# Fused expert product and quantized product: the stores of the results move from SyncE's queue to one of GpSimd's

## What is computed

```
cond = einsum('bsd,bdh->bsh', x, W[cat]) + b[cat][:, None, :]
w_scale = mean(abs(weight)) + EPS
w_quant = clip(round(weight / w_scale), -1, 1)
a_scale = max(abs(cond), axis=-1, keepdims=True) + EPS
a_quant = round(clip(cond / a_scale * 127.0, -128.0, 127.0))
out = x + einsum('bsi,oi->bso', a_quant, w_quant) * (w_scale * a_scale / 127.0)
```

## Time and profile before

| | |
|---|---|
| time, median of 3 runs | 519.17 us (518.93 to 520.29) |
| profiled execution: its own time | 519.77 us |
| profiled execution: its span | 518.0 us |
| granted TensorE clock, mean | 0.998 |
| TensorE matmul busy | 503.4 us (97%) |
| VectorE busy | 363.2 us (70%) |
| ScalarE busy | 349.3 us (67%) |
| GpSimd busy | 298.8 us (58%) |
| DMA queue q1 (all of SyncE's), share of 16 engines | 92.7% |

### The profile page before, as it was taken

The page is one execution under the profiler, slowest core; times in us unless marked ns, Lnnn a source line. Parts: engine busy times, 40 slices in busy tenths (PEclk is TensorE's granted clock), DMA queues, the critical chain, the costliest instruction groups (busy, mean ns, idle before and its releaser), DMA issues.

```text
span 518.0 us, 13961 instructions
## 1 busy us (share of the span) xinstructions
PE 503.4 (97%) x2584; PEld 361.0 (70%) x2585; DVE 363.2 (70%) x651; ACT 349.3 (67%) x504; POOL 298.8 (58%) x397
## 2 busy tenths in 40 slices
PE   4899999999999999999999999999999999999996
PEld 1576777777777777777777777777777777777773
DVE  3397854878657968766766869855978587566844
ACT  4477766776676777757756777765877667567642
POOL 3397655656646656555565556565665655655640
PEclk9999999999999999999999999999999999999999
DMA  6879989999999999999999999999999999799843
GB/s 205 293 262 334 353 308 322 379 361 351 331 360 360 409 389 402 354 302 374 363 324 322 327 371 393 394 321 346 409 391 381 337 357 358 259 339 321 304 152 120
DMA packets 71728, 172.76 MB, mean 333 GB/s; under 512 B 8096, under 2 KB 8224, under 8 KB 71584
## 3 DMA queue, kind: packets, MB, share of 16 engines
q1 hardware_dynamic: 71712, 172.59, 92.7%
HBM read 139.00 MB, written 33.55 MB: 333 GB/s over the span
## 4 chain that ended last, share of the span: by engine, by line
PE 92%; POOL 2%; DMA 2%; issue 1%; DVE 1%; ACT 1%; SPq 1%; POOLq 0%; ACTq 0%; DVEq 0%
PE ps_cond L656 22%; PE ps_cond L658 22%; PE ps_cond L657 22%; PE ps_y L624 21%; PE ps_aT L634 6%; POOL sb_y_scale L355 2%; DMA sb_w_raw<-cond_wb 1%; DMA sb_cat_row_i<-itok 1%; PE ps_y L606 0%; POOL sb_xT_hi L331 0%; POOL sb_xT_lo L336 0%; DVE sb_absmax L564 0%; ACT sb_w_hi L403 0%; ACT sb_aT L428 0%; SPq L261 0%
## 5 line engine op out<-in xcount | busy, mean ns | idle before, releaser
L336 POOL TENSOR_TENSOR sb_xT_lo<-sb_xT_raw,sb_xT_hi 128x512 fp32r<-128x512 f32 x128 | 186.4, 1456 | 193.5 <-PE ps_cond L658 192.5
L656 PE MATMUL ps_cond<-sb_w_hi,sb_xT_hi 128*128 x512 | 225.1, 440 | 0.2
L658 PE MATMUL ps_cond<-sb_w_hi,sb_xT_lo 128*128 x512 | 201.0, 393 | 0.0
L657 PE MATMUL ps_cond<-sb_w_lo,sb_xT_hi 128*128 x512 | 199.7, 390 | 0.0
L564 DVE TENSOR_REDUCE sb_absmax<-ps_cond 128x1 f32<-128x512 f32 x128 | 87.8, 686 | 126.0 <-PE ps_cond L658 125.7
L447 ACT ACTIVATE sb_a_rounded<-ps_cond,sb_rounder,sb_a_inv 128x512 f32<-128x512 f32 x128 | 99.6, 778 | 61.4 <-DVE sb_a_inv L570 61.0
L521 DVE TENSOR_TENSOR sb_w_lo<-sb_w_raw,sb_w_hi x106 | 137.2, 1333 | 0.1
L624 PE MATMUL ps_y<-sb_ffnT,sb_aT 128*128 128x512 bf16 x512 | 131.5, 380 | 1.0 <-ACT sb_aT L428 1.0
L428 ACT ACTIVATE sb_aT<-ps_aT 128x512 bf16<-128x512 int16 x128 | 75.5, 590 | 65.6 <-PE ps_aT L634 65.5
L656 PEld LDWEIGHTS ps_cond<-sb_w_hi,sb_xT_hi 128*128 128x128 f32 x512 | 96.9, 189 | 31.3 <-issue 1.9
L658 PEld LDWEIGHTS ps_cond<-sb_w_hi,sb_xT_lo 128*128 128x128 f32 x512 | 96.4, 188 | 21.8
(11 more groups left out here) (71 smaller groups left out, 37.7 us busy)
## 6 DMA issues: line engine op xcount, KB each, us to landing
sb_w_raw<-cond_wb SPq DMA_DIRECT2D x53, 768.0 KB, 7.4
sb_xT_raw<-x_t SPq DMA_DIRECT2D x128, 256.0 KB, 4.9
sb_x_rows<-x SPq DMA_DIRECT2D x128, 256.0 KB, 5.0
out<-sb_x_rows SPq DMA_DIRECT2D x128, 256.0 KB, 4.8
sb_w_raw<-cond_wb SPq DMA_DIRECT2D x53, 512.0 KB, 6.0
sb_w_raw<-cond_wb SPq DMA_DIRECT2D x5, 256.0 KB, 4.5
sb_ffn_raw<-ffn_t SPq DMA_DIRECT2D x1, 1024.0 KB, 6.9
sb_cat_row_i<-itok SPq DMA_DIRECT2D x1, 64.0 KB, 3.5
```

Of the source, the lines that this page charges most:

```text
L336: pool.tensor_tensor(xT_lo[:, m, :], xT_raw[:, m, :], xT_hi[:, m, :].bitcast(F32), ALU.subtract).then_inc(x_lo_done, 1)
L656: pe.matmul(ps_cond, x_hi_k, w_hi_k, start=False, stop=False, skip_group_check=True)
L657: pe.matmul(ps_cond, x_hi_k, w_lo_k, start=False, stop=False, skip_group_check=True)
L658: last_mm = pe.matmul(ps_cond, x_lo_k, w_hi_k, start=False, stop=(k == KD - 1), skip_group_check=True)
```

## The change

The function `store` moves from SyncE's program to GpSimd's. There it looks up its own row (one value), waits for `y_done` and issues the transfer on GpSimd's queue. It stands at the end of GpSimd's body for step r, behind `split_x_high`, and stores the result of step r-4, as before. SyncE's look-up of a step reads one value less (six for seven), and its loads follow each other. The order of GpSimd's and SyncE's other work is unchanged.

```
@@ SyncE
-            def store(element, step, n):
-
-                sp.wait_ge(y_done, step + 1)
-                sp.dma_start(out[bass.ds(element, 1), :, :].rearrange("a s o -> (a s) o"),
-                             x_rows[:, n, :]).then_inc(stored[n], 16)
-
...
             def body(r0, u, first, last):
                 r = r0 + u
-                row = row_of(sp, r + W_AHEAD, NEW, OUT_ELEMENT + 1)
-                if not first or u >= STORE_BEHIND:
-                    store(bounded(sp, row[OUT_ELEMENT], B - 1), r - STORE_BEHIND, (u - STORE_BEHIND) % U)
+                row = row_of(sp, r + W_AHEAD, NEW, ROWS_ELEMENT + 1)
...
             over_steps(sp, body)
-            for u in range(U - STORE_BEHIND, U):
-                (element,) = row_of(sp, B - U + u + STORE_BEHIND + W_AHEAD, OUT_ELEMENT, 1)
-                store(bounded(sp, element, B - 1), B - U + u, u)
@@ GpSimd
+            def store(step, n):
+                (element,) = row_of(pool, step + STORE_BEHIND + W_AHEAD, OUT_ELEMENT, 1)
+                element = bounded(pool, element, B - 1)
+
+                pool.wait_ge(y_done, step + 1)
+                pool.dma_start(out[bass.ds(element, 1), :, :].rearrange("a s o -> (a s) o"),
+                               x_rows[:, n, :]).then_inc(stored[n], 16)
+
...
                     split_x_high(r + X_AHEAD + 1, (u + X_AHEAD + 1) % U)
 
+                if not first or u >= STORE_BEHIND:
+                    store(r - STORE_BEHIND, (u - STORE_BEHIND) % U)
+
             over_steps(pool, body)
+            for u in range(U - STORE_BEHIND, U):
+                store(B - U + u, u)
```

## The result

| | before | changed |
|---|---|---|
| median, 20 executions each (us) | 520.66 | 521.97 |
| lowest to highest (us) | 518.93 to 522.70 | 520.60 to 522.78 |
| ratio, 95% interval | | 1.0028 (1.0019 to 1.0038) |
| span of the profiled execution (us) | 518.0 | 521.1 |
| granted TensorE clock, mean | 0.998 | 0.999 |

The change costs a quarter of a per cent. It is just inside the 0.3% that I called no change, but the interval excludes 1: on the median it is 1.3 us, where the forecast had 0.65 us. On the scale of the forecast it is 1.0028 x 519.17 = 520.6 us, inside the forecast's own range. The two profiled executions lie 3.1 us apart.

The account below looks back on a forecast made before the run. TensorE's gapless step of 3.85 us was taken to bound the kernel. Loop 0, start 0 and end 0.65 us on 519.77 gave 520.4 us, or 519.8 us on the median's scale of 519.17, range 518.9 to 520.7.

Parts of the forecast that it names:

- SyncE's relief: In the loop, SyncE's loads go out some 0.5 us earlier without the stores; hidden before, so costed at nothing.
- G: Time one store's transfer takes on GpSimd itself: taken as 1.0 us, bounded by 0.355 and 2.28 us.
- A: Loop: G doesn't fit and GpSimd sets the step; 532 us at G = 1.6, 613 at the upper bound; chance 0.12.
- B: Loop: VectorE's weight split holds up the transfer's list making by 2.2 us; near 545 us, 568 at most; chance 0.10.
- D: DMA: two queues share the 16 engines worse than one; some 3 us or more, 523 and up; chance 0.04.
- A step of 3.85 leaves 1.50 us: Loop: GpSimd's three operations take 2.345 us of the step, leaving 1.50 us of room for G.
- Each 0.1 us above costs 12 us: Loop: once G passes 1.5 us, every further 0.1 us is paid in 120 steps, 12 us.
- the row of 2.28 us: Start: GpSimd's row scales, 0.26 us otherwise, took 2.28 us, just to the end of VectorE's weight split.
- The start, "Cost: nothing": Start: GpSimd lags, but its low splits for steps 7 and 8 are still ready while G is under 1.8 us.
- The end is the one place where nothing covers G: End: issuing the last store from GpSimd takes 1.0 us instead of 0.35, adding 0.65 us.
- Rival C: End: with G = 1.5 and a landing 0.5 us longer, 1.65 us more, 520.8 to 521.5; chance 0.07.

Follow-up runs that it names:

- s2: The changed kernel with each store issued as two transfers of half the columns: 535.88 us, against 519.84 for the kernel before, ratio 1.0309.
- r0: The kernel before with one unused difference of two SBUF arrays added to each GpSimd body: 582.87 us against 519.84, ratio 1.1226.
- the second comparison: The changed kernel unaltered, measured again against the kernel before: 522.01 us against 520.08, ratio 1.0036.
- r1: The kernel before with an unused difference and a copy added to each GpSimd body: 644.38 us against 519.84, ratio 1.2399.

## Why the prediction was right and wrong

**The bound and the loop: right.** TensorE's step stayed at 3.85 us, what SyncE's relief brought was hidden, and G fitted. G itself was mis-sized: 0.56 us, not 1.0. My nearest row, a pass of GpSimd's cores over 128 partitions, was the wrong measure in its upper half, and the expected 0.8 to 1.3 us was missed at the low end. Look-up and wait cost GpSimd next to nothing, and rivals A, B and D didn't come: the DMA share was 0.97 from 100 to 200 us, for 1.01 before.

**"A step of 3.85 leaves 1.50 us": wrong.** It did no harm, because only 0.56 were used. But "Each 0.1 us above costs 12 us" from G = 1.5 on would have been badly off: s2 used 1.12 us and lost some 11 us ahead of its end, r0 used 1.3 us and lost 63. Had G been the 1.0 us that I took, the forecast of no change in the loop might well have failed; that wasn't run. What failed in it is the count of GpSimd's own busy time as if it were fixed; it depends on when VectorE splits a weight. In the prediction I saw this in the row of 2.28 us and drew the rival from it only for the transfer, not for the row scales and low splits that the transfer would move.

**The start, "Cost: nothing": wrong by one stall** of 0.3 to 0.9 us in four profiles. The forecast checked whether the low splits are ready in time, and they are. It costed the look-up on GpSimd alone, and did not ask what else would be late: the stall stands at TensorE's own look-up, 1.0 to 1.5 us long there. It also did not ask what the low splits would fall upon; whether the longer weight splits are behind the late look-up is not shown.

**"The end is the one place where nothing covers G": right in place, wrong in size.** The term was +0.65 us and measured +1.5 us. It had one part, the longer issue. In its place stand three: from the result to the issue 0.5 us, issue to landing 0.3 us, and the drain of GpSimd 0.7 us, which I had not looked at, since in the kernel before it was over at 510.4, long before the end. The estimate by the first-byte times of the Trainium skill, "DMA: Bandwidth & Descriptors", section "Latency and other measured facts" (about 1 against 0.6 us), was 0.4 us; by the sums above the store landed about 0.8 us later behind its result, so the measurement decides, and the drain comes on top. Giving back the last four stores took 1.4 us off. That the sum came so near is in part luck: with G at its measured 0.56 the same term would have been 0.56 - 0.355 = 0.2 us, so the G that was too large covered part of what was left out. Rival C, "Only the end grows, by more", at 520.8 to 521.5, had the right place and, by the 1.5 us of the rows, nearly the right size, with another mechanism: it took G for 1.5 us, and G was not what grew.

**The sum.** Forecast 519.8 on a median of 519.17, which is +0.65; measured +1.3 here, beside a median of 520.66 for the kernel before, and +1.9 in the second comparison. The rows give 1.5 at the end and up to 0.9 at the start.

## To carry to other kernels

Choose the engine for a program's last transfers apart from the one for the loop. A queue that costs nothing in the loop can still cost at the end: here ScalarE came late to the last stores because it had others in front of them, and GpSimd, idle by then, came late by its longer way and its drain. Four transfers of 128 given back to SyncE took most of the loss away. Look behind the last wait too, at what each engine does to close its program.

Room on an engine is not the step less its busy time when another engine can lengthen its operations. The way to find out is to add a known piece of work to the step and time it: here 0.56 us were free in the loop and 1.12 us cost about 11 us. And where a profile gives no engine as the cause of a stall, read the sequencer's own rows, such as its look-ups.

## What was not expected of the hardware

- Making the list for a store of 128 rows of 2 KB took GpSimd 0.54 to 0.76 us (0.76 for its first), 0.56 in the median, and as much again for a transfer of rows half as long (0.555 us).
- A GpSimd that has issued transfers closes with a drain of 2.5 us (1 or 4 transfers), 3.3 to 3.5 us (120 to 128) or 5.2 us (256), against 0.38 us in the kernel before. The row includes GpSimd's last operation, so it is 1.6 us in r0 and 2.1 us in r1, without any transfer. Past the landing of the last transfer it goes on for 0.1 to 0.2, 0.7 to 1.0 and 3.2 us.
- TensorE's look-up of two values from the table in SBUF took 0.54 us in the median and up to 1.46 us, and one of these, begun only 1.0 us before TensorE's work ran out, made it stand still.
- A GpSimd store starts 0.64 us behind the result that it waits for, SyncE's 0.16 us.
- One half of a weight split took VectorE 4.36 us instead of 1.33 with GpSimd reading SBUF in it, and 0.26 us of row scales on GpSimd took 2.30 us behind one.
